# Attention in a two-layer megakernel: a second pair of banks for the turned scores, the query stacks' copies on ScalarE, and the last turn ahead of an output product

## The reference

```python
q, k = _apply_rope(q, cos, sin), _apply_rope(k, cos, sin)     # 32 query heads of 16, 8 key heads
k = jnp.repeat(k, GROUPS, axis=1); v = jnp.repeat(v, GROUPS, axis=1)
logits = jnp.einsum('bhqd,bhkd->bhqk', q, k) * scale
logits = jnp.where(causal[None, None], logits, jnp.finfo(logits.dtype).min)
attn = jax.nn.softmax(logits, axis=-1)
out = jnp.einsum('bhqk,bhkd->bhqd', attn, v)
x = x + out.transpose(0, 2, 1, 3).reshape(bsz, q_len, NH * HD) @ Wo.T
```

## Time and profile before

| | us |
|---|---|
| median of 3 runs | 2438.72 |
| lowest, highest | 2435.86, 2439.78 |
| the profiled execution | 2434.77 |
| its span | 2433.0 |
| the attention stage in it | about 2077 to 2377 |

### The profile page before, as it was taken

How to read it: one execution, slowest core, us unless ns; L and a number is a source line. 1 busy time by engine, 2 the same in 40 slices (tenths; PEclk the granted TensorE clock), 3 DMA queues, 4 the chain that set the end, 5 groups by cost and what they waited for, 6 DMA issues and landing times. The chain is left out here.

```text
span 2433.0 us, 33409 instructions
## 1 busy us (share of the span) xinstructions
PE 2322.9 (95%) x12530; PEld 1799.7 (74%) x12530; DVE 1653.1 (68%) x2131; ACT 1308.2 (54%) x1911; POOL 1337.8 (55%) x879
## 2 busy tenths in 40 slices
PE   7998899999999999999999999999988998889878
PEld 6877788888888888888888888888767875545434
DVE  5556887688588578678668758858736544667624
ACT  2323776477467467567657647747732313325544
POOL 2222598599489579669759859948942220100000
PEclk9999999999999999999999999999989999999999
DMA  5422333233223233333323323323215320200001
GB/s 132 107 77 64 104 120 103 88 102 117 83 93 120 87 101 104 100 96 101 107 87 113 104 78 113 112 83 100 83 39 114 90 76 14 82 2 3 2 2 49
DMA packets 163631, 204.09 MB, mean 84 GB/s; under 512 B 24492, under 2 KB 86320, under 8 KB 163344
## 3 DMA queue, kind: packets, MB, share of 16 engines
q1 hardware_dynamic: 162096, 201.43, 28.0%
q10 hardware_dynamic: 1376, 0.53, 0.1%
HBM read 198.43 MB, written 3.15 MB: 83 GB/s over the span
## 5 line engine op out<-in xcount | busy, mean ns | idle before, releaser
L2008 POOL TENSOR_TENSOR mamba_w_lo<-mamba_raw,mamba_w_hi 128x512 fp32r<-128x512 f32 x272 | 436.1, 1612 | 282.9 <-ACT mamba_w_hi L1828 282.9
L76 PE MATMUL psum<-mamba_hT_lo,mamba_w_hi 128*128 128x512 f32 x1152 | 459.4, 399 | 1.8 <-DVE mamba_bc L2100 1.8
L78 PE MATMUL psum<-mamba_hT_hi,mamba_w_lo 128*128 128x512 f32 x1152 | 457.7, 397 | 0.0
L77 PE MATMUL psum<-mamba_hT_hi,mamba_w_hi 128*128 128x512 f32 x1152 | 454.2, 394 | 0.0
L2027 POOL TENSOR_SCALAR mamba_L<-mamba_A,mamba_ts 128x256 f32<-128x256 f32 (+1 forms) x256 | 333.9, 1318 | 0.1
L2132 DVE TENSOR_TENSOR mamba_L<-mamba_L,mamba_cb 128x1536 f32<-128x1536 f32 x128 | 302.6, 2364 | 21.6 <-ACT mamba_L L1877 15.8
L2100 DVE SCALAR_TENSOR_TENSOR mamba_hid<-psum,mamba_cw,mamba_hid 128x1022 f32<-128x1022 f32 (+2 forms) x192 | 245.2, 1277 | 19.8 <-ACT mamba_hid L1835 15.3
L77 PEld LDWEIGHTS psum<-mamba_hT_hi,mamba_w_hi 128*128 128x128 f32 x1152 | 216.5, 188 | 51.4
L76 PEld LDWEIGHTS psum<-mamba_hT_lo,mamba_w_hi 128*128 128x128 f32 x1152 | 216.5, 188 | 51.3 <-DVE mamba_bc L2100 2.0
L78 PEld LDWEIGHTS psum<-mamba_hT_hi,mamba_w_lo 128*128 128x128 f32 x1152 | 216.3, 188 | 51.5
L296 POOL TENSOR_TENSOR ffn_w_lo<-ffn_deq,ffn_w_hi 128x512 fp32r<-128x512 f32 (+2 forms) x66 | 86.2, 1307 | 268.9 <-ACT ffn_w_hi L308 268.9
(11 more groups left out here) (279 smaller groups left out, 4886.8 us busy)
## 6 DMA issues: line engine op xcount, KB each, us to landing
mamba_A<-mamba_a_dram SPq DMA_DIRECT2D x128, 512.0 KB, 4.5
mamba_raw<-in_win SPq DMA_DIRECT2D x144, 256.0 KB, 2.6
mamba_raw<-in_wout SPq DMA_DIRECT2D x128, 256.0 KB, 2.6
mamba_Eb<-mamba_e_dram SPq DMA_DIRECT2D x128, 128.0 KB, 3.0
ffn_raw<-in_w SPq DMA_DIRECT2D x80, 128.0 KB, 3.7
ffn_scl<-in_s SPq DMA_DIRECT2D x76, 128.0 KB, 3.9
ffn_scl<-in_s SPq DMA_DIRECT2D x86, 64.0 KB, 2.4
ffn_raw<-in_w SPq DMA_DIRECT2D x20, 256.0 KB, 2.7
```

The lines of the kernel that those rows point to most:

```text
L76: e.matmul(out, wh, ml, start=start, stop=False)
L77: e.matmul(out, wh, mh, start=False, stop=False)
L78: return e.matmul(out, wl, mh, start=False, stop=stop)
L2008: e.tensor_tensor(w.lo[:, k % NSPLIT, :], raw[:, k % NRAW, :], w.hi_read[:, k % NSPLIT, :], ALU.subtract).then_inc(s["w_lo"], 1)
```

## The change

1. From t = 26 (T2) on, the units use bank 0-1 alone, and score_t(t, 1) goes to banks 2 and 3. score_t then waits for the exponentials of the half before last, not of the last. Unit k from 80 (K2) on waits for peak k - 1, where it waited for k - 2.
2. `keep`: in sequence 1 ACT copies all 16 query stacks, DVE none. Keys, and sequence 0, are as before.
3. In an iteration with both, the turn "og" comes ahead of the output product if t is 40 or more (once: t = 40). The products of the last two steps go to banks 0 and 1.
4. The unread transposes at the start: 24, 18 and 8, where they were 14, 6 and 6.

```diff
+    T2 = 26
+    K2 = sum(len(us) for us in UNITS_OF[:6])
+        def kept(b, z):
+            if z % 2 and (b == 0 or z < NKV):
+                return st_dve, b * STACKS // 2 + z // 2 + 1
+            return st_act, b * STACKS // 2 + (z // 2 + 1 if b == 0 or z < NKV else NKV // 2 + z - NKV + 1)
+        def unit_bank(k):
+            return 2 * (k % 2) if k < K2 else 0
+        def pair_bank(t, m):
+            return 2 if t >= T2 and m else 4
+        def out_bank(s):
+            return 7 if s < NS - 2 else s - (NS - 2)
...
-            return out + [("og", s, j) for s in range(NS) for j in range(2) if t == ENDS[s, j] + 1]
+            turned = [("og", s, j) for s in range(NS) for j in range(2) if t == ENDS[s, j] + 1]
+            return out + (product + turned if t < TQ else turned + product)
...
                     for z in stacks_of(i):
-                        kept = st_act if z % 2 == 0 else st_dve
                         if b and z >= 2:
-                            e.wait_ge(kept, STACKS // 2 + z // 2)
+                            e.wait_ge(*kept(b, z - 2))
...
                     if k >= 2:
-                        e.wait_ge(peaked, k - 1)
-                    bank = 2 * (k % 2)
+                        e.wait_ge(peaked, k - 1 if k < K2 else k)
+                    bank = unit_bank(k)
...
-                    if k:
+                    if t == T2 and m:
+                        e.wait_ge(peaked, K2)
+                    elif t > T2 or (t == T2 and m):
+                        e.wait_ge(exped, 2 * (k - 1))
+                    elif k:
                         e.wait_ge(exped, 2 * k)
...
-                    wait_spare()
+                    if out_bank(s) == 7:
+                        wait_spare()
+                        spare[0] = (x_done, s + 1)
+                    else:
+                        e.wait_ge(peaked, UEND[-1])
...
-                keep_clock(e, ps[7], ident, 14)
+                keep_clock(e, ps[7], ident, 24)
                 for h in range(2):
                     e.wait_ge(var_ready, h + 1)
-                    keep_clock(e, ps[7], ident, 6)
+                    keep_clock(e, ps[7], ident, 18 - 10 * h)
...
                 def keep(b, i):
-                    for z in stacks_of(i)[::2]:
+                    for z in stacks_of(i):
+                        if kept(b, z)[0] is st_dve:
+                            continue
```

More of the change, by code:

```diff
@@ L887, in turns_at @@
             out = [("on", s) for s in range(NS) if t == ENDS[s, 1] + 2]
-            out += [("out", s) for s in range(NS) if t == ENDS[s, 1] + 3]
-            return out + [("og", s, j) for s in range(NS) for j in range(2) if t == ENDS[s, j] + 1]
+            product = [("out", s) for s in range(NS) if t == ENDS[s, 1] + 3]
+            turned = [("og", s, j) for s in range(NS) for j in range(2) if t == ENDS[s, j] + 1]
+            return out + (product + turned if t < TQ else turned + product)
         TEND = TQ + 3
@@ L1015, in place @@
                         elif z >= 4:
-                            e.wait_ge(kept, z // 2 - 1)
+                            e.wait_ge(*kept(b, z - 4))
                         s = QPK + z if i == 0 else (z - NKV) % QPK
@@ L1056, in score_t @@
                     z = QPK * (2 * j + m)
-                    outs = [ps[4 + h].rearrange("p (h q) -> p h q", h=QPK) for h in range(2)]
+                    outs = [ps[pair_bank(t, m) + h].rearrange("p (h q) -> p h q", h=QPK) for h in range(2)]
                     for h in range(2):
@@ L1103, in out_product @@
                     e.wait_ge(wo_in, 16)
-                    wait_spare()
+                    if out_bank(s) == 7:
[3 more added lines that the diff above has]
+                        e.wait_ge(peaked, UEND[-1])
                     for a in range(DT):
-                        last = e.matmul(ps[7], oT[:, a, :], wo[:, a, :], start=a == 0, stop=a == DT - 1)
+                        last = e.matmul(ps[out_bank(s)], oT[:, a, :], wo[:, a, :], start=a == 0, stop=a == DT - 1)
                     last.then_inc(out_mm, 1)
-                    spare[0] = (x_done, s + 1)
-                keep_clock(e, ps[7], ident, 14)
+                keep_clock(e, ps[7], ident, 24)
                 for h in range(2):
                     e.wait_ge(var_ready, h + 1)
-                    keep_clock(e, ps[7], ident, 6)
+                    keep_clock(e, ps[7], ident, 18 - 10 * h)
                 for t in range(HALF_T):
@@ L1126, in _ @@
                         place(0, i - 2)
-                e.wait_ge(st_act, STACKS // 2)
-                e.wait_ge(st_dve, STACKS // 2)
+                e.wait_ge(*kept(0, STACKS - 2))
+                e.wait_ge(*kept(0, STACKS - 1))
                 e.wait_ge(mask_ready, 4)
@@ L1141, in _ @@
                     if i == NR + 2:
-                        e.wait_ge(st_act, SEQS * STACKS // 2)
-                        e.wait_ge(st_dve, SEQS * STACKS // 2)
+                        e.wait_ge(*kept(1, STACKS - 1))
+                        e.wait_ge(*kept(1, NKV - 1))
                         e.wait_ge(neg_in[1], 32)
@@ L1211, in exponential @@
                         e.wait_ge(pv, (k - NPT) // 4 + 1)
-                    e.activation(pt[:, k % NPT, :], ps[4 + i % 2], ACT.Exp, scale=SCALE).then_inc(exped, 1)
+                    e.activation(pt[:, k % NPT, :], ps[pair_bank(t, i // 2) + i % 2], ACT.Exp, scale=SCALE).then_inc(exped, 1)
                 def take_out(s, j):
@@ L1280, in keep @@
                 def keep(b, i):
-                    for z in stacks_of(i)[1::2]:
+                    for z in stacks_of(i):
+                        if kept(b, z)[0] is st_act:
+                            continue
                         e.wait_ge(placed, b * STACKS + z + 1)
@@ L1290, in peak @@
                     e.tensor_reduce(mx[:, s % 2, :].rearrange("p (h z) -> p h z", h=2)[:, :, z:z + DEEP[s]],
-                                    psum[:, 2 * (k % 2):2 * (k % 2) + 2, 0:DEEP[s] * n].rearrange("p h (y n) -> p h y n", y=DEEP[s]),
+                                    psum[:, unit_bank(k):unit_bank(k) + 2, 0:DEEP[s] * n].rearrange("p h (y n) -> p h y n", y=DEEP[s]),
                                     AX.X, ALU.max).then_inc(peaked, 1)
@@ L1314, in add_out @@
                     xt = x[:, b * QT + qt, :]
-                    e.tensor_tensor(xt, xt, ps[7], ALU.add).then_inc(x_done, 1)
+                    e.tensor_tensor(xt, xt, ps[out_bank(s)], ALU.add).then_inc(x_done, 1)
                 for h in range(2):
```

## The result

Beside four runs of the kernel before (median 2439.05 us) four runs of the changed kernel gave 2421.04 us (2418.4 to 2422.76): ratio 0.9931, 95% interval 0.9915 to 0.9948. That is faster than the forecast of 2428.1 and outside its range, 2423.6 to 2433.5. With all runs of this document together the kernel before stands at 2435.9 in the mean of 79 (standard deviation 3.8) and the changed one at 2420.0 in the mean of 10 (2.3). So 15.9 us were gained where 10.6 were forecast; of the 18 between the first medians, 2 us were chance.

A forecast was written before the change was run, and what follows sets the result against it. The bound was taken to be score_t waiting for ACT's exponentials, since both halves share banks 4 and 5. Savings of 0.1 + 1.0 + 9.5 = 10.6 us from 2438.72 gave 2428.1 us, range 2423.6 to 2433.5.

The forecast's parts named there:

- the circle through ACT: From t = 26, score_t, exponentials, weigh, next score_t: 2.67 us without mask, 2.90 with it; 8.4 us saved.
- the transfer held quad 28: Quad 28 would wait for its maxima's transfer, 1.8 us plus 0.15 wake-up, leaving TensorE idle 0.7 us.
- The order at t = 40: At the attention stage's end, turn og ahead of the output product and banks 0 and 1 would save 1.1 us.
- The copies: In sequence 1, ACT copying all query stacks would shorten the wait before each group's last stack: 1.0 us saved.
- comes or goes: A low stretch of TensorE's clock, as in placing sequence 1, would move a run by up to 1.7 us.
- The start: More unread transposes would speed the first turns by some 1.3 us; 0.1 saved, bounds 0.2 saved and 1.2 lost.
- The wait for `sel`: ACT's first projection copy would still wait for POOL's cast until 2096.17, absorbing almost all the faster turns gain.
- The base: Starting time for the forecast: 2438.72 us, the kernel before's median of three runs, 3.95 above the profiled execution.
- Rival (d): Short idle times in the new order drop the clock for the whole stretch: 27 us slower, 2466; chance 0.03.
- (a): The second pair of banks buys nothing while units are there, quads 26 to 33: 2434.0 us; chance 0.10.
- (b): ACT becomes the bound in the projections, its added copies losing 3.9 us: 2433.0 us; chance 0.05.
- Rival (c): Quad 28's transfer takes 3.2 us instead of 1.8: 9.2 saved, 2429.5 us; no separate chance, within the forecast's range.

The follow-up runs named there:

- the waits filled: Kernel before with only twelve unread transposes added at each wait for a group's first stack copy in sequence 1: 2430.87 us, ratio 0.9988.
- the part alone: Kernel before with only the unread transposes at the start raised to 24, 18 and 8: 2436.81 us, ratio 1.0003.
- part 1 alone: Kernel before with only the second pair of banks from quad 26 on and units from 80 on in one pair: 2429.79 us, ratio 0.9979.
- two fillings: Changed kernel plus twelve unread transposes at each group's first-copy wait in sequence 1 and eight ahead of the first quad: 2418.82 us, ratio 0.9935.

## Why the prediction was wrong

**The end of the circle through ACT (part 1): right, to a tenth of a us.** Counted from quad 26, quads 28, 34, 36 and 38 were forecast at 6.96, 30.19, 35.85 and 44.15 us and came at 7.06, 30.26, 35.85 and 44.25. weigh took the wait over in the quads without units, and the transfer held quad 28, both as put; the quad started 1.99 behind the transfer's issue, put at 1.8 + 0.15. The runs give this part 6.1 +- 0.8, the traces 8.2. That gap is 2.7 standard errors, hard to call chance, and no trace shows where the 2 us went.

**The order at t = 40 (part 3): mechanism right, size low.** 1.5 us in the traces, not 1.1, because the product follows the turn in 0.49 (put at 0.59), "on" the product in 3.44 (3.63) and the last product "on" in 1.27 (1.40). The rest up to 3.5 +- 0.8 I didn't forecast at all. Two of six traces without this part had a low stretch over the last product, costing 1.5 and 2.9 us by the length of the stage; with it none of eight. Were the stretch as frequent either way, such a split would still come about one time in six: the clock's share here is not shown.

**The copies (part 2): the mis-sized term.** Forecast 1.0 us, from the wait in front of stack 11. Without low clock the traces give 51.8 - 50.6 = 1.2, so the work was right. The runs give 4.8 +- 0.8. What failed is the term that the sum put at nothing, the clock: the sentence that a low stretch "comes or goes" and moves a run by up to 1.7 us, as if it were noise that stays out of the comparison. By these runs its frequency goes with the kernel. With DVE's copies three of five traces had two low stretches 84 to 101 us into the stage, which made a query projection 4.8 and 5.2 us long instead of 3.6, or the value projections and the placing slower. With ACT's copies, or the waits filled, none of nine. If they were equally frequent in all, such a split would come about one time in 36, and the place was picked after seeing the traces. The means of the lists with and without part 2 (unfilled) differ by 3.0 us (54.0 and 51.0), not 1.2. The filled kernel speaks for the clock as the cause: it leaves the copies as before, hands nothing to ACT and does no work earlier, yet its trace has no stretch there and its time is 2.9 us lower, in an interval that just reaches zero. One trace and that interval support the cause; together with the counts I take it as likely, not as proved. What in the groups brings the stretches stays open as well. Part 2 leaves the wait of 1.72 for the first copy and takes out only the 0.27 ahead of the group's last stack; the filling takes out 1.3 of the first wait and leaves the 0.27. Both were followed by no stretch there.

**The start (part 4): about right in the mean, wrong in kind.** Forecast 0.1, with bounds of 1.2 lost and 0.2 gained. Measured 1.1 +- 0.8 by the fit, nothing by the part alone. The wait for `sel` hides what the turns gain, as forecast. But where the clock was low under the first projection as well, that cover was gone and the start took 2.4 us more (trace of part 1 alone). The bound of 0.2 came from the one execution that was profiled. Two things in the table were not forecast either. With the longer filling the first 16 us have 1.7 us at the low clock in the mean of eight traces, without it 7.4 in six. And the stretch in the first quads, which costs up to 2.6 us, came in six of the eight and in one of the six, so that first quad to quad 26 is 0.8 us longer in the mean (114.1 and 113.3), about what the start gains (0.9). That part 4 brings it is not shown, but it would explain why the part alone gave nothing. (The forecast also read all 20 first transposes as run at the low clock; the trace before has full clock from 2080.4 on, under the last four.)

**The base.** The forecast was set from the median of three, 2438.72. Over 79 runs the kernel before has a mean of 2435.9. That error, 2.8 us, made the forecast slower still: against the mean of 79 the same sum would have given 2425.3, still 5 us too slow.

**Rival (d), the clock, had the right subject and the wrong sign.** I asked only whether the second pair of banks could bring low stretches: of fourteen traces, eight with the second pair and six without, none had one between quad 26 and the end of the second last product, some 60 to 70 us. So the rule of the Trainium skill that the forecast weighed there (TensorE: Matmul & The Clock Gate, "A second HAM failure mode: psum-queue depth-cycling") has no case in that part of these traces. I didn't ask whether the waits of before brought them elsewhere. Rivals (a) and (b) fell: quads 26 to 33 saved what they should, and part 2 lost nothing. Rival (c) did not happen: quad 28's wait was 0.65, and 1.08 in the trace with two fillings.

What stays open: the segments' means give 8.2 + 3.0 + 1.5 (2.2 with the stretches at the end) + 0.9 for part 4, 13.6 to 14.3 us, and the runs 15.9 with a standard error of 0.8. The last 2 us or so are not assigned, and part by part the two ledgers differ by as much: part 1 less by the runs, parts 2 and 3 more. Neither is it known what brings the stretch in the first quads (seven of fourteen traces, 2.2 to 2.6 us where it lasts 6.8); it was there with and without each part.

## What to carry to other kernels

A group of short waits on TensorE may be priced twice: by itself, and by the chance that a stretch of half clock falls on the work behind it. Part 2 was worth 1.2 us by its waits, 3.0 by the traces and 4.8 +- 0.8 by the runs. A single profile shows one draw of that chance; before forecasting small gains, count the low stretches in several traces, and set the base from many runs. A wait that can't be removed can be filled: twelve unread transposes a group gave about 2.9 us in the kernel before, in an interval that reaches zero, and nothing that could be told in the changed one.

## What was not expected of the hardware

- Idle times of TensorE of 1.7 us each, four within 30 us, were followed by the 1.2 GHz level in three of five traces; the same place with waits of 0.4 us (three traces), or with waits of 1.7 and the groups 0.27 us shorter (six), never.
- In the attention stage the level fell for 3.4, 6.8 or 10.2 us at a time. A projection of eight matmuls took 4.8 to 5.4 us in it for 3.6 to 3.7, the last product 5.16 and 6.27.
- Stages that no edit touches differ between executions: the last stage took 50.7 to 51.2 us without a low stretch of 6.8 us and 54.2 to 54.3 with it, and the stages ahead of attention differed by 4.7 us.
